# Latent attention in a decoder kernel: shift transposes behind the last score tiles, the next batch's parts split sooner, each batch's result stored within the last stage

## The reference

```python
xn = layer_norm(ctx, g1, b1)                 # 8 x 1024 x 256
ln = layer_norm(layernorm(x), g2, b2)        # 8 x 512 x 256
k, v = split(concatenate([xn, ln], axis=1) @ Wkv)   # 1536 keys per batch
q = ln @ Wq
w = softmax((q / 64**.25) @ (k / 64**.25).T)        # per batch and head
x = x + (w @ v) @ Wout
gate = silu(bitlinear(x, w_gate)); up = bitlinear(x, w_up)
x = x + bitlinear(gate * up, w_down)         # result, 4 MB
```

## Time and profile before

| | |
|---|---|
| time, three runs | 5628.34 us median, 5625.23 to 5630.53 us |
| profiled execution, its own time | 5628.69 us |
| its span, first to last instruction | 5626.9 us |
| span of latent attention | some 2960 to 5345 us |
| feed-forward phase | to some 5612 us |
| final store | to the end of the span |
| TensorE, VectorE, ScalarE, GpSimd busy, of the span | 89%, 68%, 51%, 44% |

### The profile page before, as it was taken

How to read it: one execution, slowest core, us unless ns; L and a number is a source line. 1 busy time by engine, 2 the same in 40 slices (tenths; PEclk the granted TensorE clock), 3 DMA queues, 4 the chain that set the end, 5 groups by cost and what they waited for, 6 DMA issues and landing times. The chain is left out here.

```text
span 5626.9 us, 84687 instructions
## 1 busy us (share of the span) xinstructions
PE 5010.0 (89%) x23756; PEld 2567.5 (46%) x23756; DVE 3847.2 (68%) x7722; ACT 2856.4 (51%) x6162; POOL 2473.3 (44%) x1470
## 2 busy tenths in 40 slices
PE   5699998599999989799949999999999999999955
PEld 3455555223333356433325555555555555555423
DVE  6666665788888657788855666666666666666587
ACT  3476666147677733266734444444444444444422
POOL 3455554300000011100026777777777777777700
PEclk9799999789999979899969999999999999999977
DMA  4476766332222100823333333333333333333100
GB/s 128 146 252 241 246 239 215 111 97 67 67 66 67 37 0 0 275 64 72 75 122 91 83 80 94 91 90 83 81 94 91 90 78 89 91 94 79 49 23 30
DMA packets 392161, 575.15 MB, mean 102 GB/s; under 512 B 35856, under 2 KB 251216, under 8 KB 390800
## 3 DMA queue, kind: packets, MB, share of 16 engines
q1 hardware_dynamic: 389136, 566.60, 36.0%
q10 hardware_dynamic: 2688, 4.46, 0.2%
HBM read 316.93 MB, written 220.20 MB: 95 GB/s over the span
## 5 line engine op out<-in xcount | busy, mean ns | idle before, releaser
L2315 POOL TENSOR_TENSOR la_acc<-la_acc,la_pr 128x1024 f32<-128x1024 f32 x704 | 1684.4, 2393 | 515.9 <-ACT la_pr L2273 446.6
L2273 ACT ACTIVATE la_pr<-la_s_ps 128x512 f32<-128x512 f32 x1536 | 793.3, 604 | 890.7 <-PE la_s_ps L2126 889.0
L2133 PE MATMUL la_o_ps<-la_pr,la_vf 128*64 128x512 f32 x3072 | 743.8, 605 | 0.0
L1519 DVE TENSOR_REDUCE ca_mx<-ca_m_ps 128x1 f32<-128x512 f32 x1024 | 639.1, 683 | 94.7 <-PE ca_m_ps L1337 90.5
L2125 PE MATMUL la_s_ps<-la_q_hl,la_k_hh 128*128 128x512 f32 x1536 | 668.2, 435 | 38.5 <-ACT la_pr L2273 31.9
L1490 ACT ACTIVATE ca_pr<-ca_s_ps 128x512 f32<-128x512 f32 x1024 | 540.9, 599 | 221.1 <-PE ca_s_ps L1352 216.3
L2126 PE MATMUL la_s_ps<-la_q_hs,la_k_l 65*128 65x512 f32 x1536 | 608.4, 396 | 0.0
L2342 DVE TENSOR_REDUCE la_mx<-la_m_ps 128x2 f32<-128x1024 f32 x384 | 463.0, 1206 | 211.4 <-PE la_m_ps L2108 207.7
L2342 DVE TENSOR_REDUCE la_mx<-la_misc 128x2 f32<-128x1024 f32 x384 | 466.3, 1214 | 0.0
L107 POOL TENSOR_TENSOR ff_ln_var_eps<-ff_ln_mv,g_eps 128x4 f32<-128x4 f32 x32 | 6.7, 209 | 1009.9 <-DVE ff_ln_mv L92 1009.9
L1337 PE MATMUL ca_m_ps<-ca_ks,ca_qs 96*128 96x512 bf16 x1024 | 403.4, 395 | 4.9 <-DVE ca_mx L1519 4.9
(11 more groups left out here) (368 smaller groups left out, 8602.6 us busy)
## 6 DMA issues: line engine op xcount, KB each, us to landing
la_k_hh<-scratch_k_high SPq DMA_DIRECT2D x128, 512.0 KB, 6.5
scratch_xv<-sc_v_full SPq DMA_DIRECT2D x128, 256.0 KB, 2.6
scratch_k_high<-sc_k_high SPq DMA_DIRECT2D x128, 256.0 KB, 2.6
scratch_k_low<-sc_k_low SPq DMA_DIRECT2D x128, 256.0 KB, 3.0
la_w_parts<-scratch_w_parts SPq DMA_DIRECT2D x64, 512.0 KB, 6.2
la_k_l<-scratch_k_low SPq DMA_DIRECT2D x64, 512.0 KB, 8.5
la_vf<-scratch_xv SPq DMA_DIRECT2D x64, 512.0 KB, 4.1
ca_ks<-scratch_kstack SPq DMA_DIRECT2D x64, 384.0 KB, 6.1
```

The lines of the kernel that those rows point to most:

```text
L1519: dve.tensor_reduce(mx[:, u % 2, qt, h, half:half + 1], m_ps[:, turn_of(u, i, NM)[0], :], AX.X, ALU.max).then_inc(m_reduced, 1)
L2133: last = pe.matmul(o_ps[XD * h:XD * h + XD, :], vf[:, par, st, XD * h:XD * h + XD], pr[:, st % LAG, h, :], start=(st == 0), stop=(st == XT ...
L2273: act.activation(pr[:, st % LAG, h, :], s_ps[:, (2 * st + h) % 3, :], ACT.Exp, scale=scale).then_inc(p_done, 1)
L2315: pool.tensor_tensor(total, total, exps, ALU.add).then_inc(acc_done, 1)
```

## The change

Four things are changed. `SHIFT` becomes 5, and on TensorE `shifts` moves from behind the `weigh` products of its round to behind the round's scores; VectorE's `negate` stays in round 4 (`max(LEAD)` is 4). ScalarE's `split_high` moves from behind round 5 to behind round 3 of the unit with `p` = 6, and VectorE's `split_low` from behind round 5 to the end of round 4. The phase `store` is dropped; SyncE stores each batch's 512 KB from within the feed-forward phase when its last tile is finished. The pieces below come in this order: the constants, TensorE, ScalarE, VectorE, SyncE.

```diff
-    SUMS, VALUES, SHIFT, OUT, INVERTS = 0, 1, 4, 5, 4
+    SUMS, VALUES, SHIFT, OUT, INVERTS = 0, 1, 5, 5, 4
...
-        def splits_next(b, p, st):
+        def splits_next(b, p):
-            return (not isinstance(b, int) or b < B - 1) and (p, st) == (XPAIRS - 2, ROUNDS - 1)
+            return (not isinstance(b, int) or b < B - 1) and p == XPAIRS - 2
...
+                        if m == SHIFT and has_next:
+                            shifts(unit + 1)
...
-                        if m == SHIFT and has_next:
-                            shifts(unit + 1)
...
-                        if splits_next(b, p, m):
+                        if m == 3 and splits_next(b, p):
                             split_high(b + 1)
...
-                        if m == SHIFT and has_next:
+                        if m == max(LEAD) and has_next:
                             negate(unit + 1)
-                        if m == SHIFT and has_prev:
+                        if m == INVERTS and has_prev:
                             normalise(unit - 1)
+                        if m == INVERTS and splits_next(b, p):
+                            split_low(b + 1)
...
-                        if splits_next(b, p, m):
-                            split_low(b + 1)
...
+                for b in range(B):
+                    sp.wait_ge(x_done, NT * (b + 1))
+                    sp.dma_start(io["out"][b].rearrange("(j p) d -> p j d", p=P), g.x[:, b * NT:(b + 1) * NT, :]).then_inc(out_stored, 16)
+                sp.wait_ge(out_stored, 16 * B)
...
-def store(nc, io, g, semctx):
...
-            sp.dma_start(io["out"].rearrange("b (j p) d -> p (b j) d", p=P), g.x[:, :, :]).then_inc(stored, 16)
-            sp.wait_ge(stored, 16)
...
-        phase(nc, io, g, store)
```

More of the change, by code:

```diff
@@ L2449, in ternary_ffn @@
         (setup, sum_ready, w_done, xstep, xround, xq_done, tp_ready, xT_done, g_ready, u_ready, gated_done, h_done,
-         hstep, hr_done, hq_done, ht_ready, hT_done, y_ready, x_done) = sems(
+         hstep, hr_done, hq_done, ht_ready, hT_done, y_ready, x_done, out_stored) = sems(
             nc, semctx, "tf", "setup sum_ready w_done xstep xround xq_done tp_ready xT_done g_ready u_ready gated_done h_done "
-            "hstep hr_done hq_done ht_ready hT_done y_ready x_done")
+            "hstep hr_done hq_done ht_ready hT_done y_ready x_done out_stored")
         HSTEPS = 4
```

## The result

The changed kernel takes 5597.55 us (median of 4 runs, 5593.23 to 5603.46) against 5629.43 us of the kernel before in the same comparison; the ratio is 0.9945, with a 95% interval of 0.9928 to 0.9962. It is 32 us faster. The forecast was 54 us less, and the range ended at 5592.

A forecast was written before the change was run, and what follows sets the result against it. TensorE was taken to bound the latent attention and VectorE to lead the feed-forward phase. Shift 39.1, split 3.5 and store 11.2 us sum to 53.8 us less, 5574.5 us from a median of 5628.34; range 5568 to 5592.

The forecast's parts named there:

- The copies are hidden, barely; cost nothing: Latent attention, round 5: ScalarE's two shift row copies end before TensorE's `project_out` needs their bank; cost nothing.
- The shift's gain: Latent attention, 63 units: moving the shift saves 0.62 us a unit, 39.1 us in all, ends 23.3 to 41.0.
- the cheap end of 0.41: Round 5: lowest cost in us assumed for the four transposes between scores and `weigh`; 0.44 taken, 0.69 the dearer end.
- Who waits for the shift now: Round 5: row copies end at 4.12 us, `project_out` comes at 4.48 us after the first score; nobody waits.
- a margin of 0.36 us: Round 5: time between the end of ScalarE's row copies and TensorE reaching `project_out`; the signal takes some 0.1.
- The split: Latent attention: earlier `split_low` and `split_high` end TensorE's 7 waits, 3.5 us gained, ends 0 and 3.8.
- The store: End of the feed-forward phase: only the last batch's 512 KB follow the last addition, 11.2 us less, ends 7.7 and 11.7.
- The sum: Whole kernel: 39.1 + 3.5 + 11.2 = 53.8 us less, giving a predicted 5574.5 us.
- the sign of being wrong: Latent attention: prediction is wrong if it is less than 25 us shorter, or if the unit's other rounds grow.
- GpSimd was no bound: Rival, latent attention: GpSimd or another engine takes over and it stays as long; 5614 to 5617 us, chance 0.04.
- the transposes were cheap: Against the rival, round 5: transposes cost 0.69 us, not 0.44, or copies come late; 38.0 us less, 5590, chance 0.13.
- `project_out` didn't wait: Against the rival, round 5: TensorE waits longer at `project_out` for the copies; slower, 5653 at 1.5 us late, chance 0.02.

The follow-up runs named there:

- e4_other_bank: The changed kernel with the transposed shifts in a bank `project_out` doesn't write, without TensorE's wait for the row copies ahead of `project_out`; 5579.61 us, ratio 0.9908.

## Why the prediction was wrong

- **The step that failed** is the prediction's "The copies are hidden, barely; cost nothing". Ahead of it stands a half reading of the list of waits: it took the entries that name an engine and passed over "issue", 13.7 us in 11 places, all of them at the jumps. That was a cost that depended on what surrounded it, and no term of the sum and no rival had the jump in it. What bounds the kernel between the jumps was read rightly.
- **The shift's gain** was right, and a little over the 41.0 at the end of its range: 0.70 us a unit, 44 us, where 0.62 and 39.1 were forecast. The transposes cost 0.36 us in their new place (4.40 less the 4.04 of a round without them), below the cheap end of 0.41.
- **Who waits for the shift now** was right for the array and wrong for the queue. The copies were hidden: `project_out` starts on time. But the prediction priced the wait for the array alone, by a margin of 0.36 us, and didn't ask what the queue does meanwhile. The queue reached the jump 2.0 us later, behind the loads. The term that stood at nothing was 31 us: the loss beside the jumps went from 20.2 to 50.9. The wait on the copies is 19.9 of that, by `e4_other_bank`; the other 10.8 came with the shift's move too and stay without the wait.
- How the 31 divides, by the twelve units' loss in the traces: from 50.9 the later loads take off 32.6 (to 18.3), the sooner start alone 19.9 (to 31.0), both together 46.8 (to 4.1). The two overlap, in part by the clock: it fell behind all six pauses of the changed kernel (14.8 us in the units behind them), behind two with late loads (2.7 us), and behind none with both.
- **The split** was right alone as far as the runs can tell: 3.5 forecast, 3.4 by medians, with an interval that takes in no change. Beside the shift it also kept the wait from growing to 7.7 us, which the prediction hadn't seen.
- **The store** was right: 11.2 forecast; 11.3 from the trace (15.2 to 3.9) and 11.8 by medians of the store alone.
- **The sum.** In the two traces the latent attention is 17.5 us shorter (2426.0 to 2408.5), near 44 + 3.7 - 31, and under the 25 us that the prediction named as the sign of being wrong. With the store's 11.3 that makes 29, beside the 32 of the medians. The traces differ by 35.5 us, but 7.6 of these lie ahead of the latent attention, where nothing was changed; they are scatter between executions.
- **The rivals.** None of them was it. GpSimd was no bound, the transposes were cheap, `project_out` didn't wait.

What stays open: why a jump without traffic takes 3.3 to 3.9 us and now and then 5, how the queues' 8 KB and 16 KB fetches divide over the engines, and why a jump 0.4 us behind the loads' start takes 6 us where one at their start takes 3.5 to 3.9; no run was made on these.

## What to carry to other kernels

A loop that spans several engines' long bodies has a price at its jump, and that price depends on how far the queue is ahead of its engine and on what the DMA engines carry at that moment. When a wait is moved, ask not only whether the array will stand still, but also what the queue would have done behind it. And an "issue" entry in the list of waits is a place to look at first, since an edit elsewhere can make it grow. Here SyncE's later wait and another PSUM bank, a few lines, were worth 43 us on top of a change worth 32.

## What the runs showed of the hardware

- A jump back on TensorE's queue takes 3.3 to 3.9 us with quiet DMA engines (one took 5.0), 7.2 to 7.9 us when 1.5 MB of loads had been issued 2.0 us before (one took 5.5; with the shift alone 4.6 to 9.1), and 6.1 to 7.0 us with as much other traffic. A jump not taken costs 83 ns. The Trainium skill, "Runtime: NRT & Kernel Launch", Instruction fetch mechanics, says that a taken branch out of the window of fetched code forces a DMA fetch before execution goes on. The traces agree. They add that the jump is longer beside data transfers: in the changed kernel a 16 KB fetch started over 4 us after it.
- ScalarE's and VectorE's jump instructions take 45 to 72 ns, but the loop's first instruction follows late: on ScalarE 2.4 to 2.7 us behind with late loads and 5.0 to 5.4 us in the changed kernel, on VectorE 2.7 to 3.0 and 6.1 to 7.2 us. On GpSimd it is 0.2 to 0.3 us in both.
- TensorE's queue jumped some 0.45 us behind the last score product before and 2.46 us behind it after, with the array's work the same: the lead of the queue hides part of the fetch, and a wait that the array never feels uses it up.
- After a pause of 5.9 us the granted clock was at 1.2 GHz, and score products came 0.43 us apart in place of 0.23. In the kernel before, behind a pause of 2.3 us at the same place, it stayed at 2.4 GHz. Behind the changed kernel's six pauses the lower clock cost 14.8 us.
- Four transposes of 128 columns between the scores and `weigh` cost 0.36 us, and 0.41 us between `weigh` and the scores.
